# Turning the attention probabilities with VectorE block transposes and two DMA passes, in a one-core decoder layer

## The chip, the cores and the metric

One core of a Trainium2 chip runs the whole layer. The metric is the device time of one execution in microseconds (us), the median of several. The engines are TensorE (PE in the profile; its weight loads are PEld), VectorE (DVE), ScalarE (ACT), GpSimd (POOL) and SyncE (SP), which issues most of the DMAs.

## The reference

The layer is a selective scan over 128 positions, then a cross attention, then a linear layer, each behind a layer norm and with a residual. The change lies in the cross attention, with 8 batches, 128 queries, 128 keys, 32 heads of width 128 and a model width of 512:

```
h_q = (rmsnorm(z) @ w_q.T)      # z: the normed rows, 8 x 128 x 512
h_k, h_v = ctx @ w_k.T, ctx @ w_v.T
score = einsum('bqhd,bkhd->bhqk', h_q, h_k) + position_bias
score = softmax(where(mask, score, -inf))
attn  = einsum('bhqk,bkhd->bqhd', where(mask, score, 0), h_v)
out   = z + attn @ w_out.T
```

## The kernel before

**Two phases.** In the first some 380 us the scan runs on VectorE, ScalarE and GpSimd, while TensorE makes K and V of all heads and SyncE stores them in DRAM (k_dram, v_dram). The attention follows, and then the linear layer of some 25 us.

**Attention steps.** The attention is 64 steps: 32 heads times two halves of four batches (HB = 4, so a tile is 128 x 512). Head number g of these 64 is worked on over several steps, and each engine runs `step(g, ...)` in order. SyncE loads K and bias of g+1 (k_sb, bias, line 482), then V and the output weights of g (v_sb, wo_raw, line 485). TensorE makes the scores of g-1 (line 754), turns the probabilities of g-2 (line 778), adds the output product of g-3 to `misc` (lines 782 to 795: twelve 512-column matmuls, three for each product, since every float32 operand is split into a high and a low part), and multiplies V with the turned probabilities of g-2 (line 809). The matmul P.V contracts over the keys, so the probabilities, which softmax leaves with queries on the partitions, must stand with keys on the partitions. TensorE does this with four 128 x 128 transposes into the PSUM bank psT, and VectorE copies the bank to pt_sb (line 1344).

**Queries.** From step 10 on the query product is done for two heads at a time with seven half-size products instead of eight (`product`, six matmuls each, lines 686 to 688): W12, S2, S1 and S4 in an even step, S3, W11 and W22 in an odd one. Two PSUM areas, sumX and sumY, take turns, and VectorE and ScalarE combine them: q_u (u_sum), q_w (w_sum), and the four quarters of the queries c11 (ScalarE, line 1099), c12 (line 1366), c22 (line 1328) and c21 (line 1369). TensorE waits for c12 ahead of the scores of an odd step, and for c21 ahead of the product S2 of an even step.

**VectorE in one step.** q_u or c22; scores plus bias (line 1334, sb_done); maximum (line 1336); q_w; copy of the turned bank (line 1344); reciprocal of ScalarE's sum (line 1358); normalising (line 1360, p_ready); c12 or c21; low part of the head's output (line 1372, ot_lo).

**The others.** ScalarE takes c11, splits the weights (line 1104; line 1108 in odd steps; line 1084 for wo_hi), does four exponentials (line 1120), and last the high part of the head's output (line 1127, ot_hi) behind P.V. GpSimd makes the sums and low parts of the query weights (lines 1590 to 1605), the masked bias bm (line 1615) and wo_lo (line 1619).

## Time and profile before

| | |
|---|---|
| median of 3 runs | 909.33 us (909.28 to 910.69) |
| the profiled execution | 907.23 us, with a span of 905.4 us |
| PE busy | 896.5 us, 99% of the span |
| PEld, DVE, ACT, POOL busy | 86%, 77%, 57%, 74% of the span |
| granted TensorE clock | 1.00 throughout |
| DMA | 150.32 MB, mean 166 GB/s |

The span is the time from the first to the last instruction. An engine's busy share is a mean over stages; which engine sets the pace of a stage is read from who waits for whom.

### The profile page before, as it was taken

To read this page: it belongs to the slowest core of one execution; us is meant where nothing else is said; L and a number is where in the kernel's file an instruction comes from. 1 tells how busy PE (TensorE), PEld (TensorE's weight loads), DVE (VectorE), ACT (ScalarE), POOL (GpSimd) and SP (SyncE) were. 2 spreads that over 40 slices of the span, in tenths; PEclk is the share of its full clock that TensorE was granted. 3 is DMA by queue.
4 is the path that set the end of the run, shared out by engine and by line. 5 is a ranking of instruction groups with operands and counts; after the bars stand their busy time and mean duration, and the time that the engine had idled before them with its cause. 6 is when DMAs were issued, how large, how long until landed. Compare 5 with 4: busy or idle time off the path is not lost.

```text
span 905.4 us, 15443 instructions
## 1 busy us (share of the span) xinstructions
PE 896.5 (99%) x5146; PEld 776.4 (86%) x5146; DVE 694.7 (77%) x757; ACT 520.2 (57%) x1198; POOL 670.8 (74%) x437
## 2 busy tenths in 40 slices
PE   8999999999999999999999999999999999999998
PEld 7687888788888888888899999999899999999876
DVE  4799899999999997475666767676667676767774
ACT  3787867665666765456555555555555555555330
POOL 3245989997678795566788787888987878787522
PEclk9999999999999999999999999999999999999999
DMA  9454767576686762457445444444454544444302
GB/s 304 174 168 146 201 200 207 185 216 207 193 281 191 240 198 96 145 172 243 161 147 161 137 158 143 152 146 153 131 166 135 160 136 160 140 156 138 98 1 94
DMA packets 96913, 150.32 MB, mean 166 GB/s; under 512 B 10608, under 2 KB 35312, under 8 KB 96736
## 3 DMA queue, kind: packets, MB, share of 16 engines
q1 hardware_dynamic: 86496, 131.60, 44.4%
q10 hardware_dynamic: 10368, 18.09, 7.7%
q8 instruction: 28, 0.46, 0.2%
q14 instruction: 21, 0.17, 0.1%
HBM read 113.88 MB, written 35.78 MB: 165 GB/s over the span
## 4 chain that ended last, share of the span: by engine, by line
PE 85%; POOL 7%; DVE 4%; issue 2%; DMA 1%; ACT 1%; SPq 0%; ACTq 0%; DVEq 0%; POOLq 0%
PE acc L522 10%; PE acc L524 10%; PE acc L523 10%; PE misc L522 6%; PE misc L523 6%; PE misc L524 6%; PE acc L754 6%; PE acc L809 6%; PE acc L686 5%; PE acc L688 5%; PE acc L687 5%; PE acc L778 3%; POOL y L1538 2%; POOL wv_lo L1500 2%; DVE misc L1268 1%
## 5 line engine op out<-in xcount | busy, mean ns | idle before, releaser
L1538 POOL TENSOR_TENSOR y<-y,w 128x2048 f32<-128x2048 f32 x31 | 143.5, 4629 | 34.9 <-DVE w L1275 31.1
L1268 DVE TENSOR_TENSOR_SCAN misc<-dA,misc 128x2048 f32<-128x2048 f32 x32 | 141.7, 4429 | 4.9 <-ACT dA L881 1.7
L1120 ACT ACTIVATE prob<-prob,negm 128x128 f32<-128x128 f32 x256 | 99.9, 392 | 43.6 <-DVE negm L1336 43.6
L1127 ACT ACTIVATE ot_hi<-acc 128x512 fp32r<-128x512 f32 x64 | 38.3, 599 | 143.5 <-PE acc L809 143.5
L1602 POOL TENSOR_TENSOR wt_lo<-ws,wt_hi 128x1024 fp32r<-128x1024 f32 x27 | 65.2, 2414 | 61.6 <-ACT wt_hi L1108 59.4
L522 PE MATMUL misc<-wo_hi,ot_hi 128*128 128x512 f32 x256 | 107.3, 419 | 0.0
L522 PE MATMUL acc<-wv_hi,ctx_hi 128*128 128x512 f32 x256 | 100.4, 392 | 1.4 <-POOL wv_lo L1500 1.4
L524 PE MATMUL misc<-wo_hi,ot_lo 128*128 128x512 f32 x256 | 101.2, 395 | 0.0
L523 PE MATMUL misc<-wo_lo,ot_hi 128*128 128x512 f32 x256 | 101.1, 395 | 0.0
L1619 POOL TENSOR_TENSOR wo_lo<-wo_raw,wo_hi 128x512 fp32r<-128x512 f32 x64 | 95.9, 1499 | 6.3 <-ACT wo_hi L1084 6.3
L524 PE MATMUL acc<-wv_hi,ctx_lo 128*128 128x512 f32 x256 | 99.8, 390 | 0.0
L523 PE MATMUL acc<-wv_lo,ctx_hi 128*128 128x512 f32 x256 | 99.8, 390 | 0.0
L522 PE MATMUL acc<-ctx_hi,wk_hi 128*128 128x512 f32 x240 | 94.8, 395 | 0.0
L524 PE MATMUL acc<-ctx_hi,wk_lo 128*128 128x512 f32 x240 | 93.7, 390 | 0.0
L523 PE MATMUL acc<-ctx_lo,wk_hi 128*128 128x512 f32 x240 | 93.5, 390 | 0.0
L1360 DVE TENSOR_TENSOR prob<-prob,rec 128x512 f32<-128x512 f32 x64 | 88.6, 1384 | 2.2
L881 ACT ACTIVATE dA<-dt_,negA 128x508 f32<-128x508 f32 x128 | 89.2, 713 | 0.4 <-ACT xp_sb L996 0.4
L1372 DVE TENSOR_TENSOR ot_lo<-acc,ot_hi 128x512 fp32r<-128x512 f32 x64 | 44.3, 692 | 54.3 <-ACT ot_hi L1127 54.2
L1615 POOL TENSOR_TENSOR bm<-bias,maskadd 128x512 f32<-128x512 f32 x64 | 78.4, 1226 | 0.0
L1263 DVE TENSOR_TENSOR misc<-u,acc 128x2048 f32<-128x2048 f32 x32 | 73.5, 2297 | 4.9 <-ACT acc L897 1.7
L1275 DVE TENSOR_TENSOR w<-misc,bc 128x2048 f32<-128x2048 f32 x32 | 73.3, 2291 | 4.1
L859 ACT ACTIVATE kst<-acc 128x512 f32<-128x512 f32 x64 | 38.0, 598 | 60.6 <-PE acc L524 44.3
(206 smaller groups left out, 2448.2 us busy)
## 6 DMA issues: line engine op xcount, KB each, us to landing
k_scratch<-kst SPq DMA_DIRECT2D x64, 256.0 KB, 3.7
bc<-xp_scratch ACTq DMA_DIRECT2D x32, 512.0 KB, 5.6
v_scratch<-vst SPq DMA_DIRECT2D x32, 512.0 KB, 3.6
k_sb<-k_scratch SPq DMA_DIRECT2D x64, 256.0 KB, 2.7
v_sb<-v_scratch SPq DMA_DIRECT2D x64, 256.0 KB, 2.7
wo_raw<-in_wo SPq DMA_DIRECT2D x64, 256.0 KB, 2.9
wp<-in_wq SPq DMA_DIRECT2D x54, 256.0 KB, 3.7
wraw<-in_wk SPq DMA_DIRECT2D x32, 256.0 KB, 4.8
```

Source lines behind the costliest of these rows:

```text
L522: pe.matmul(out, w_hi, m_hi, start=first, stop=False)
L523: pe.matmul(out, w_hi, m_lo, start=False, stop=False)
L524: return pe.matmul(out, w_lo, m_hi, start=False, stop=last)
L881: act.activation(dA[k % 2][:, c, :, 1:S], dt_[:, half, c, :, 1:S], ACT.Exp, scale=negA[:, c, n:n + 1]).then_inc(da_ready, 1)
L1120: last = act.activation(prob[q][:, b], prob[q][:, b], ACT.Exp, bias=negm[q][:, b:b + 1], accum_out=psum[q][:, b:b + 1])
L1263: dve.tensor_tensor(misc[:, :, :], cols(u[:, half]), every(b_ps), ALU.mult).then_inc(dbx_done, 1)
L1268: dve.tensor_tensor_scan(h_ps, flat(dA[k % 2][:, :, :, :]), h_ps, 0.0, ALU.mult, ALU.add).then_inc(da_free, 1)
L1275: dve.tensor_tensor(cols(w[:, k % 2]), misc[:, :, :], every(bc[k % TRI][:, 1]), ALU.mult).then_inc(prod_done, 1)
L1360: dve.tensor_tensor(prob[q][:], prob[q][:], rec[q][:, :].unsqueeze(2).to_broadcast([P, HB, S]), ALU.mult).then_inc(p_ready, 1)
L1538: pool.tensor_tensor(y_half(half), y_half(half), w[:, k % 2], ALU.add).then_inc(y_ready, 1)
L1615: pool.tensor_tensor(bm[p][:], bias[p][:, :].unsqueeze(1).to_broadcast([P, HB, S]), maskadd[:, sh * HB:(sh + 1) * HB], ALU.add).then_inc(b ...
L1619: pool.tensor_tensor(wo_lo[p][:], wo_raw[p][:], wo_hi[p][:].bitcast(F32), ALU.subtract).then_inc(wo_lo_done, 1)
```

## The change

What it does:

- TensorE's four transposes (t_done), and VectorE's copy of their bank (pt_evac), go.
- Right behind normalising, VectorE transposes the 128 x 512 tile of probabilities in blocks of 32 x 32 within each group of 32 partitions (`turn`), into a new tile `blocks`.
- SyncE writes `blocks` to DRAM (one DMA of 256 KB) at the start of a step, ahead of the step's other loads. Behind the load of K and bias it waits for the write to have landed, and then reads it back with four DMAs of 64 KB, each into 32 partitions of pt_sb, in rows of 512 bytes, so that the blocks come to their transposed places.
- V and wo_raw are loaded one step later (for g-1).
- P.V moves one step later (g-3) and from the end of a step to a place ahead of the output product, which moves one step later too (g-4). ot_hi, ot_lo, split_wo and wo_lo follow. The pipeline has one step more at its end (STEPS + 4 steps).
- In an even step the product W12 now stands ahead of S2.
- The loads of the linear layer's weights go from SyncE at steps 4 to 6 to ScalarE's queue at steps 28 to 37. o_sum shares the memory of ea_sb. The transposes of the linear layer's first half (f_input) stand behind the output product of step 66 instead of at its start.

```diff
@@ SyncE, step
+                if runs(g - 2):
+                    sp.wait_ge(turned, g - 1)
+                    sp.dma_start(p_dram[p].rearrange("q j k x -> (q j) k x"),
+                                 blocks[p][:, :, :, :].rearrange("p k b i -> p k (b i)")).then_inc(blocks_out[p], 16)
...
                     load_kb(g + 1, head(g + 1, half), 1 - p)
-                if runs(g):
-                    if not known(g) or g >= 2:
-                        sp.wait_ge(pv_done, g - 1)
-                    sp.dma_start(v_sb[p][:, :, :].rearrange("p b d -> p (b d)"), v_dram[g]).then_inc(v_in[p], 16)
-                    if not known(g) or g >= 2:
-                        sp.wait_ge(wo_lo_done, g - 1)
-                    sp.dma_start(wo_raw[p][:], a["wo"][head(g, half)]).then_inc(wo_in[p], 16)
...
+                if runs(g - 2):
+                    sp.wait_ge(blocks_out[p], in_count(g - 2, p, 16))
+                    for k in range(4):
+                        sp.dma_start(pt_sb[p][32 * k:32 * (k + 1), :, :, :].rearrange("j q b i -> j q (b i)"),
+                                     p_dram[p, :, :, k].rearrange("q j x -> j q x")).then_inc(pt_in[p], 16)
+                if runs(g - 1):
+                    if not known(g) or g >= 3:
+                        sp.wait_ge(pv_done, g - 2)
+                    sp.dma_start(v_sb[1 - p][:, :, :].rearrange("p b d -> p (b d)"), v_dram[g - 1]).then_inc(v_in[1 - p], 16)
+                    if not known(g) or g >= 3:
+                        sp.wait_ge(wo_lo_done, g - 2)
+                    sp.dma_start(wo_raw[1 - p][:], a["wo"][(g - 1) % H if known(g) else g - 1 - H * half]).then_inc(wo_in[1 - p], 16)
@@ TensorE, step
                 elif paired(i) and not p:
+                    pe.wait_ge(s1_done, count(i))
+                    product(sumX, W12, pp, *z_of(half, 1, 0), False).then_inc(p2_done, 1)
                     pe.wait_ge(wc_lo, count(i))
                     if not known(i) or i > FIRST_PAIR:
                         pe.wait_ge(c21_done, count(i) - 1)
                     product(sumY, S2, pp, *t_of(half, T2), True).then_inc(p6_done, 1)
-                    pe.wait_ge(s1_done, count(i))
-                    product(sumX, W12, pp, *z_of(half, 1, 0), False).then_inc(p2_done, 1)
...
-                if runs(g - 2):
-                    pe.wait_ge(p_ready, g - 1)
...
-                    for b in range(HB):
-                        mm = pe.transpose(psT[:, b * S:(b + 1) * S], prob[p][:, b], ident[:])
-                    mm.then_inc(t_done, 1)
...
                 if runs(g - 3):
+                    pv(g - 3, 1 - p)
+                if runs(g - 4):
...
-                    pe.wait_ge(ot_lo_done, g - 2)
-                    pe.wait_ge(wo_lo_done, g - 2)
+                    pe.wait_ge(ot_lo_done, g - 3)
+                    pe.wait_ge(wo_lo_done, g - 3)
...
+            def pv(h, p):
+                pe.wait_ge(pt_in[p], in_count(h, p, 64))
+                pe.wait_ge(v_in[p], in_count(h, p, 16))
+                if known(h) and h == 0:
+                    pe.wait_ge(sum_evac, slot(NG, 0) - 1)
+                else:
+                    pe.wait_ge(ot_lo_done, h)
+                for b in range(HB):
+                    mm = pe.matmul(psO[:, b * S:(b + 1) * S].rearrange("p (q i) -> p q i", q=4), v_sb[p][:, b],
+                                   pt_sb[p][:, :, b], start=True, stop=True)
+                mm.then_inc(pv_done, 1)
@@ VectorE, step
-                    dve.tensor_copy(pt_sb[p][:, :, :].rearrange("p b q -> p (b q)"), psT).then_inc(pt_evac, 1)
...
                                       ALU.mult).then_inc(p_ready, 1)
+                    turn(g - 1, q)
...
+            def turn(h, q):
+                dve.wait_ge(p_ready, h + 1)
+                if not known(h) or h >= 2:
+                    dve.wait_ge(blocks_out[q], in_count(h - 2, q, 16))
+                dve.transpose(blocks[q][:, :, :, :].rearrange("p k b i -> p b k i"),
+                              prob[q][:, :, :].rearrange("p b (k j) -> p b k j", j=32)).then_inc(turned, 1)
```

## Rows read from the trace of the kernel before

**Rows 1.** Window: busy us of PE, PEld, DVE, ACT, POOL; clock; DMA share; GB/s.

```profile
700.00:800.00 100.00, 100.00 (x710) 92.87 (x710) 69.62 (x115) 53.90 (x166) 83.31 (x75) 1.00 0.49 153
```

**Rows 2.** Timeline of TensorE, one even and one odd step: start, duration in us.

```profile
720.87 0.36 PE L686 MATMUL acc<-tz,wt_hi 128*128 128x256 f32 x1
...
722.39 1.05 PE L754 MATMUL acc<-k_sb,q_sb 128*128 128x128 f32 x8
...
723.99 0.60 PE L778 MATMUL acc<-ident,prob 128*128 128x128 f32 x4
724.35 0.48 PE L522 MATMUL misc<-wo_hi,ot_hi 128*128 128x512 f32 x1
...
727.93 1.05 PE L809 MATMUL acc<-pt_sb,v_sb 128*128 128x128 f32 x8
728.74 0.36 PE L686 MATMUL acc<-tz,wt_hi 128*128 128x256 f32 x1
...
729.53 1.05 PE L754 MATMUL acc<-k_sb,q_sb 128*128 128x128 f32 x8
...
735.89 0.36 PE L686 MATMUL acc<-tz,wt_hi 128*128 128x256 f32 x1
```

**Rows 3.** Waits, 500 to 860 us: total us, times, longest us.

```profile
ACT ot_hi L1127 <- PE acc L809: 113.8, 48, 2.5
POOL wt_lo L1602 <- ACT wt_hi L1108: 54.4, 22, 2.6
```

**Rows 4.** Timeline of VectorE, an odd step and the even one behind it.

```profile
718.95 1.44 DVE L1360 TENSOR_TENSOR prob<-prob,rec 128x512 f32<-128x512 f32 x1
720.31 0.41 DVE L1369 TENSOR_TENSOR q_sb<-acc,q_s 128x256 f32<-128x256 f32 x1
...
723.48 0.69 DVE L1334 TENSOR_TENSOR prob<-acc,bm 128x512 f32<-128x512 f32 x1 [0.67 <-PE acc L754]
...
726.83 1.77 DVE L1360 TENSOR_TENSOR prob<-prob,rec 128x512 f32<-128x512 f32 x1
728.52 0.41 DVE L1366 TENSOR_TENSOR q_sb<-acc,q_u 128x256 f32<-128x256 f32 x1
```

**Rows 5.** Timeline of GpSimd in the same steps.

```profile
715.62 2.40 POOL L1602 TENSOR_TENSOR wt_lo<-ws,wt_hi 128x1024 fp32r<-128x1024 f32 x1 [2.58 <-ACT wt_hi L1108]
...
718.67 1.16 POOL L1615 TENSOR_TENSOR bm<-bias,maskadd 128x512 f32<-128x512 f32 x1
...
721.49 0.74 POOL L1590 TENSOR_TENSOR ws<-wp 128x256 f32<-128x256 f32 x1
...
726.76 1.29 POOL L1619 TENSOR_TENSOR wo_lo<-wo_raw,wo_hi 128x512 fp32r<-128x512 f32 x1
```

**Rows 6.** Two lines of VectorE: ns min/median/max, first and last start.

```profile
L1336 DVE TENSOR_REDUCE negm<-prob x64: 685/686/689, 384.6 to 859.3; 128x4 f32<-128x512 f32 x64
...
L1360 DVE TENSOR_TENSOR prob<-prob,rec x64: 691/1441/1814, 387.2 to 862.5; 128x512 f32<-128x512 f32 x64
```

**Rows 7.** Issue to landing: K's store (line 395, 256 KB), bias load (line 445, 64 KB).

```profile
DMA to landing us min/median/max: 2.0/3.7/8.4
...
DMA to landing us min/median/max: 2.2/3.0/6.3
```

**Rows 8.** Timeline of SyncE's queue: loads of K and bias.

```profile
724.34 0.33 SPq L444 DMA_DIRECT2D k_sb<-k_scratch  x1
724.87 0.33 SPq L445 DMA_DIRECT2D bias<-in_pbias  x1
```

**Rows 9.** Windows around the loads of V and wo_raw, and of K and bias.

```profile
721.00:724.30 3.30, 3.30 (x31) 3.30 (x30) 1.81 (x4) 2.31 (x5) 3.22 (x5) 1.00 0.48 159
724.30:729.00 4.70, 4.70 (x31) 4.16 (x30) 3.80 (x6) 1.67 (x9) 3.75 (x4) 1.00 0.25 70
```

**Rows 10.** Timeline of TensorE at the end: a weight sum, the linear layer's start.

```profile
866.91 1.98 PE L699 MATMUL acc<-eb_sb,ea_sb 128*128 128x512 f32 x4 [0.34 <-DVE ffn_w L1385]
...
877.30 0.39 PE L522 MATMUL acc<-weff_hi,zf_hi 128*128 128x512 f32 x1
```

More of the change, by code:

```diff
@@ L210, in decoder_layer @@
         prob = [sb(whole, f"prob{i}", [P, HB, S]) for i in pair]
-        pt_sb = [sb(whole, f"pt_sb{i}", [P, HB, S]) for i in pair]
+        pt_sb = [sb(whole, f"pt_sb{i}", [P, 4, HB, 32]) for i in pair]
         bm = [sb(whole, f"bm{i}", [P, HB, S]) for i in pair]
@@ L215, in decoder_layer @@
         ffn_w = sb(whole, "ffn_w", [P, C, D])
-        o_sum = sb(whole, "o_sum", [P, 2, D])
+        blocks = [sb(whole, f"blocks{i}", [P, 4, HB, 32]) for i in pair]
+        o_sum = ea_sb
         with ExitStack() as second_raw:
@@ L717, in step @@
                     weff_sum_of(2 * (g - STEPS))
-                if known(g) and g == STEPS + 2:
-                    f_input(0, (weff_sum, C), (sb_done, STEPS), (c21_done, count(PAIRS - 1)), (ot_lo_done, STEPS))
                 if plain(g):
@@ L795, in step @@
                     mm.then_inc(o_done, 1)
+                if known(g) and g == STEPS + 2:
+                    f_input(0, (weff_sum, C), (sb_done, STEPS), (c21_done, count(PAIRS - 1)), (ot_lo_done, STEPS))
                 if paired(i) and not p:
@@ L804, in step @@
                     v_sum(NG - 1, B - 1)
-                if runs(g - 2):
-                    pe.wait_ge(pt_evac, g - 1)
-                    pe.wait_ge(v_in[p], in_count(g - 2, p, 16))
-                    for b in range(HB):
-                        mm = pe.matmul(psO[:, b * S:(b + 1) * S], v_sb[p][:, b], pt_sb[p][:, b], start=True, stop=True)
-                    mm.then_inc(pv_done, 1)
+            def pv(h, p):
[9 more added lines that the diff above has]
+                mm.then_inc(pv_done, 1)
             def behind(g):
@@ L1122, in step @@
                     last.then_inc(exp_done, 1)
-                if runs(g - 2):
-                    act.wait_ge(pv_done, g - 1)
-                    if not known(g) or g > 3:
-                        act.wait_ge(o_done, g - 3)
-                    act.activation(ot_hi[p][:], psO, ACT.Copy).then_inc(ot_hi_done, 1)
+                if runs(g - 3):
+                    act.wait_ge(pv_done, g - 2)
+                    if not known(g) or g > 4:
+                        act.wait_ge(o_done, g - 4)
+                    act.activation(ot_hi[1 - p][:], psO, ACT.Copy).then_inc(ot_hi_done, 1)
+                if known(g) and H - 4 <= g < H:
+                    c = g - H + 4
+                    act.dma_start(ffn_w[:, c], a["ffn_w"][:, c]).then_inc(ffn_in, 16)
+                if known(g) and g == H:
+                    act.dma_start(ffn_b[:], a["ffn_b"].partition_broadcast(P)).then_inc(ffn_in, 16)
+                if known(g) and g == H + 5:
+                    act.wait_ge(x2_pool, 2)
+                    act.dma_start(ea_sb[:], a["ffn_a"]).then_inc(ffn_in, 16)
+                if known(g) and g == H + 1:
+                    act.dma_start(eb_sb[:], a["ffn_bw"]).then_inc(ffn_in, 16)
+                    for e in range(ER):
+                        act.dma_start(eprob[:, e:e + 1], a["probs"][P * e:P * (e + 1), :]).then_inc(ffn_in, 16)
                 if known(g) and g == STEPS:
```

65 lines of the change are left out of this document (25 added, 40 removed).

## The prediction

> **What bounds the kernel now.** I read three things in turn. First the busy time of a stretch of the attention [rows 1]: TensorE is busy for 100.00 of 100 us at the full clock, and VectorE (69.62) and GpSimd (83.31) are not. So a matmul that goes shortens the attention, as long as nothing else takes its place. Second the timeline of TensorE [rows 2], for what each block costs in pace and how long a pair of steps is: from 720.87, where an even step begins with the product S2, to 735.89, where the next one does, it is 15.02 us. Twenty-seven such pairs (heads 10 to 63) and ten heads of the plain form make up the attention. Third the timelines of VectorE and GpSimd [rows 4, 5], for how close behind TensorE the results come that it needs. They come very close. VectorE's c21 ends at 720.31 + 0.41 = 720.72, and TensorE uses it at 720.87. Its c12 ends at 728.52 + 0.41 = 728.93, and TensorE uses it at 729.53. The change makes TensorE quicker and puts work on VectorE just ahead of c12 and c21, so these two distances decide.
>
> **What TensorE saves.** The four transposes take 723.99 to 724.35, that is 0.36 us, and the matmul behind such a block of 128-column float32 matmuls takes 0.48 instead of 0.39 us, some 0.08 more [rows 2, 10]. P.V takes the transposes' place in front of the output product and pays the 0.08 there, but no longer does so in front of the next step. So a step saves 0.44 us, 64 steps save 28.2 us, and a pair would take 15.02 - 0.88 = 14.14 us. This is the most that the change can give, and one end of the range: 909.3 - 28.2 = 881.1 us.
>
> **What VectorE gets.** The trace has no block transpose. The nearest row is the maximum over the same 128 x 512 tile in SBUF, one source: 686 ns, with 685 and 689 as extremes, so GpSimd doesn't disturb it [rows 6]. The far bound is normalising, the same tile with two sources: 1,441 ns in the median [rows 6]. Below 0.69 us nothing on VectorE handles this many elements in float32 from these rows. I take 0.69, since it has one source. The copy that goes was off the path: it lay in the time of the exponentials. The Trainium skill, VectorE: DVE Perf Modes, The three transpose paths, gives 311 ns for a 128 x 128 bf16 transpose on VectorE; with three more tiles at one element per cycle of 0.96 GHz an estimate by that page is 0.71 us, and the sum would be the same within 0.02 us a step.
>
> **The two chains.** Chain A runs from the start of an even step's scores to the odd step's scores, through bias, maximum, exponentials, normalising and c12. Before, it takes VectorE 728.93 - 722.39 = 6.54 us and TensorE arrives after 7.14 us [rows 2, 4]. Chain B runs from the odd step's scores (729.53 - 15.02 = 714.51) to c21: 6.21 us, and TensorE arrives at S2 after 6.36 us.
> Now TensorE arrives on A after 7.14 - 0.44 = 6.70 us. On B it loses the transposes (0.36) and gains the product W12, which moves in front of S2: (1.52 - 0.08) / 2 = 0.72 us from 720.87 to 722.39; so 6.72 us. A, B and S2 (0.71) together are 14.13 us, which agrees with 14.14.
> With `turn` (0.69) and a hand-over of 0.07 us (VectorE starts 0.04 us behind the scores' end at 723.44 [rows 2, 4]; back to TensorE I allow a little more), A would take VectorE 7.30 us, 0.60 too long, and B 6.97 us, 0.25 too long. If nothing else changed, the saving would be gone: 14.13 + 0.85 = 14.98 us a pair.
>
> **Normalising gets shorter.** It takes 0.69 us alone (the shortest of 64) and 1.44 or 1.77 us here [rows 4, 6]. What is added is the rest of the GpSimd instruction that runs when it starts: it starts at 726.83, wo_lo ends at 728.05, and 0.69 later is 728.74 against an observed 728.60; in the odd step bm ends at 719.83, and 0.69 later is 720.52 against 720.39 [rows 4, 5]. So what counts is what GpSimd does then, and that shifts. Before, ScalarE waits up to 2.5 us for P.V with ot_hi, and behind it GpSimd waits up to 2.6 us for the split weights (L1602) [rows 3]. Now P.V of an even step begins 1.60 us behind its scores (where the transposes were, 723.99 - 722.39) and is over long before the exponentials, which end some 0.2 us ahead of normalising, 4.2 us behind the scores. From the end of P.V (728.98) to L1602 (715.62 + 15.02 = 730.64) it is 1.66 us, ot_hi and the split; counted from the exponentials' end L1602 starts at 4.2 + 1.66 = 5.9 instead of 8.25 us behind the even scores. From L1602 to the end of the odd step's wo_lo it is 3.05 + 1.16 + 1.29, so that ends at 11.4. The odd normalising starts at 6.72 + 4.44 = 11.16 and takes about 1.0 us. Then GpSimd, held off for 0.7, does what lay between 721.49 and 728.05 (6.56 us), and ends at 18.7, that is 4.3 us behind the next even scores: normalising there starts at 4.44 and takes about 0.7 us.
> Then A is 6.54 - 1.77 + 0.7 + 0.69 + 0.07 = 6.23 (needed after 6.70) and B is 6.21 - 1.44 + 1.0 + 0.69 + 0.07 = 6.53 (needed after 6.72). Both are covered by TensorE. What stays is thin: c12 must now wait for S4, which ends right in front of S3, so its 0.17 of matmul tail, 0.41 of work and hand-overs lie against the 0.71 of S3, and c21 stands the same way against W22 and W12. And GpSimd's place is known to some 0.3 us. I take a stall of 0.05 on A and 0.15 on B: 14.33 us a pair, 0.69 saved.
>
> **DMA.** A step gets one write of 256 KB and four reads of 64 KB. The turned odd head is ready at 11.16 + 1.0 + 0.69 = 12.9. The write is first in SyncE's step, where it waits for VectorE only; the query weights and K queued behind it aren't due, since K waits for sb_done at 14.33 + 1.09 + 0.69 = 16.1 anyway. It lands between 2.0 and 3.7 us later [rows 7], so by 16.7. K and bias are issued at 16.1 and 16.6, and the reads at 0.53 us each [rows 8], 17.2 to 18.8. The last lands 3.0 us later [rows 7], at 21.8. P.V of that head is at 14.33 + 6.72 + 1.60 = 22.65, so 0.9 us are left, and 0.2 if a read takes 3.7. V and wo_raw come behind, by 20.4, for a P.V more than a step later. The engines' load: K or V or wo_raw takes 0.48 x 3.3 / 2 = 0.79 us of all 16, K and bias 0.25 x 4.7 = 1.18, so 64 KB in 512-byte rows 0.39 [rows 9]. Added are 0.79 + 4 x 0.39 = 2.35 us to some 0.47 x 7.5 = 3.5, 5.85 of 7.17 us: 82%, busy but not full. I cost DMA at nothing; cover gone, each 0.1 us that a read is late beyond the 0.9 costs a pair 0.1.
>
> **Start, end and the rest.** The plain steps have no c12 or c21 and save the full 0.44 each: 4.4 us. P.V one step later makes the pipeline deeper, which moves work from the start to the end and adds none. At the end the last head's way from scores through the write (2.0 to 3.7) and reads (1.6 + 3.0) takes 4.44 + 1.0 + 0.69 + 2.0 to 3.7 + 4.6, 12.7 to 14.4 us. Beside it stand two P.V (0.80), two output products (2.9) and three weight sums of some 1.5 us [rows 2, 10], 12 us. So it costs 1 to 2 us; I take 1. The moved loads of the linear layer take ScalarE, which is half idle, a few issues.
>
> **Sum.** 27 x 0.69 + 4.4 - 1 = 22.0 us. Against the profiled execution, 907.2 becomes 885.2 and the span 905.4 becomes 883.4; the median of the runs lies 2.1 us above that execution, so I predict 887.3 us.
>
> **Rivals.**
> *Normalising stays as long.* For it: GpSimd is busy 83%, and in a shorter pair over 90%, so it is easy to meet. Against: the shift worked out above. A pair takes 14.98 us, and 27 x 0.04 + 4.4 - 1 = 4.5 us are saved: 904.8.
> *The reads land late.* For it: 0.9 us of room, and a queue that gets fuller, with reads behind K. Against: medians, not extremes, fill the room. With reads 1.5 us late each pair waits 0.6: 27 x 0.09 + 3.4 = 5.8 saved, 903.5. From 1.8 us late on it is slower than before.
> *The block transpose is dear (slower than before).* At normalising's 1.44 us, with normalising short, A misses by 0.28 and B by 0.56, a pair takes 14.97, and it is 905. With normalising as long as before A misses by 1.35 and B by 1.0: 16.5 us a pair, 27 x 1.46 - 3.4 = 36 us slower, 945. The turning point is 0.77 us per transpose with long normalising, 1.5 us with short. For it: no row of VectorE shows a float32 tile crossing partitions. Against: the 0.69 of every one-source row. In the same page of the Trainium skill, Rules for kernel authors gives TensorE the 128 x 128 transpose and VectorE only the 32 x 32 one; by that rule the change would go this way, and no row here shows it.
>
> **Chances.** The forecast (881 to 896) 0.50, normalising as long 0.14, late reads 0.16 (of it 0.05 slower), a dear transpose 0.17 (of it 0.11 slower), something not seen 0.03. What a measurement here tells from no change is 0.2%, 1.8 us. Faster 0.78, same 0.05, slower 0.17. The range reaches from the full saving, 880, to 911, beyond the two rivals at 905. The forecast's own is 881 to 896.
>
> **What would show it.** Right: no line for the transposes; `turn` at some 690 ns; line 1360 at a median under 1.1 us; a pair of 14.1 to 14.5 us; ScalarE's wait for P.V gone; reads that land ahead of P.V. Wrong: TensorE waiting for c21 (S2) or c12 (odd scores) by 0.5 us or more, which is the long normalising or a long `turn`, or waiting ahead of P.V for pt_sb.

## The result, and the profile after

The changed kernel takes 904.99 us (median of 6 runs, 903.06 to 906.27), the kernel before in the same comparison 909.31: a ratio of 0.9952, with a 95% interval of 0.9939 to 0.9965. It is faster, but by 4.3 us where 22.0 were predicted. The profiled execution took 903.9 us, its span is 902.1 us against 905.4.

The window that [rows 1] shows of before, 700 to 800 us, in the same columns:

```profile
700.00:800.00 100.00, 98.84 (x667) 89.69 (x665) 62.76 (x117) 54.67 (x174) 83.66 (x76) 1.00 0.72 221
```

TensorE is no longer busy all the time: 1.16 us of 100 are idle. The clock is full. The DMA share went from 0.49 to 0.72. The parts of VectorE's work that the prediction priced, from the lines of the changed kernel (ns min/median/max):

```profile
L1369 DVE TENSOR_TENSOR prob<-prob,rec x64: 691/694/1822, 386.9 to 856.2; 128x512 f32<-128x512 f32 x64
...
L1389 DVE STREAM_TRANSPOSE blocks<-prob x64: 711/711/716, 387.6 to 858.0; 128x512 f32<-128x512 f32 x64
```

The block transpose costs 0.71 us, and normalising fell from a median of 1.44 [rows 6] to 0.69. Both are as forecast. The wait of ScalarE for P.V [rows 3] is no longer among the waits over 1.4 us of that stretch. What waits from 500 to 860 us:

```profile
POOL wt_lo L1620 <- ACT wt_hi L1110: 34.1, 21, 1.9
...
PE acc L810 <- DMA pt_sb<-p_scratch: 3.5, 4, 1.7
...
PE acc L754 <- issue: 2.8, 11, 0.7
```

No row says that TensorE waits for VectorE's c12. Yet the pair is long. TensorE's timeline over an odd head's scores (705.10), the even step's end and the next scores (712.20):

```profile
704.32 0.35 PE L688 MATMUL acc<-tz,wt_hi 128*128 128x256 f32 x1
...
705.10 1.05 PE L754 MATMUL acc<-k_sb,q_sb 128*128 128x128 f32 x8
...
706.70 1.05 PE L810 MATMUL acc<-pt_sb,v_sb 128*128 128x128 f32 x8
707.51 0.47 PE L524 MATMUL misc<-wo_hi,ot_hi 128*128 128x512 f32 x1
...
710.39 0.27 PE L688 MATMUL acc<-z_hi,wt_hi 128*128 128x256 f32 x1
...
710.98 0.28 PE L690 MATMUL acc<-z_hi,wt_lo 128*128 128x256 f32 x1
711.10 0.28 PE L688 MATMUL acc<-tz,wt_hi 128*128 128x256 f32 x1
...
711.69 0.28 PE L690 MATMUL acc<-tz,wt_lo 128*128 128x256 f32 x1
712.20 0.80 PE L754 MATMUL acc<-k_sb,q_sb 128*128 128x128 f32 x5 [0.23 <-issue]
```

The same stretch on VectorE, from the even step's normalising on:

```profile
709.63 0.69 DVE L1369 TENSOR_TENSOR prob<-prob,rec 128x512 f32<-128x512 f32 x1
710.47 0.71 DVE L1389 STREAM_TRANSPOSE blocks<-prob 128x512 f32<-128x512 f32 x1
711.39 0.42 DVE L1376 TENSOR_TENSOR q_sb<-acc,q_u 128x256 f32<-128x256 f32 x1 [0.20 <-PE acc L690]
```

S4 (the row at 710.98 is its last) ends at 711.26, the transpose at 711.18. c12 (L1376) starts behind both, at 711.39, and ends at 711.81. S3, from 711.10, is all that TensorE has meanwhile; its last matmul starts at 711.69 and hands the array on after 0.12. The scores start at 712.20, 0.39 after c12. From 705.10 to 712.20 are 7.10 us, where TensorE's own work is 6.70 and 6.75 were predicted. The pair from 697.52 to 712.20 is 14.68 us; over ten pairs, from the scores of head 40 (682.86) to those of head 60 (829.21), it is 14.64 on average, against 15.02 before and 14.33 predicted. The short steps (chain A) are 6.98 to 7.10 there but for one of 6.72, the long ones (chain B and S2) mostly 7.58 to 7.68, where 7.58 were predicted. So what is too long is mainly A.

The start of the pipeline is worse. P.V of head 1, in step 4:

```profile
405.65 2.08 PE L810 MATMUL acc<-pt_sb,v_sb 128*128 128x128 f32 x8 [4.11 <-DMA pt_sb<-p_scratch]
407.38 0.77 PE L524 MATMUL misc<-wo_hi,ot_hi 128*128 128x512 f32 x1
...
408.80 0.63 PE L524 MATMUL misc<-wo_hi,ot_hi 128*128 128x512 f32 x1
...
411.24 0.39 PE L524 MATMUL misc<-wo_hi,ot_hi 128*128 128x512 f32 x1
```

TensorE waits 4.11 us for the reads, and then its matmuls take 0.63 instead of 0.39 us until 411. Windows of that stretch (the clock is the third figure from the end):

```profile
404.00:406.00 2.00, 0.35 (x1) 0.35 (x2) 2.00 (x2) 0.00 (x0) 2.00 (x2) 0.57 0.59 170
406.00:408.00 2.00, 2.00 (x10) 1.90 (x10) 1.39 (x3) 0.54 (x3) 1.23 (x1) 0.50 1.02 280
408.00:410.00 2.00, 2.00 (x6) 1.60 (x5) 0.82 (x2) 2.00 (x8) 0.00 (x0) 0.50 0.85 314
```

The granted clock is 0.50 there, the level of 1.2 GHz. P.V and nine matmuls take 405.65 to 411.24, 5.59 us; the same in a steady step (706.70 to 709.69) takes 2.99. So the low clock costs 2.6 us beside the wait.

**Where the 18.7 us of span are that are missing.** Between the scores of head 10 (457.84 before, 457.83 after) and those of the last head (857.52, 851.50) 6.0 us were saved. The forecast for these 26.5 pairs was 26.5 x 0.69 = 18.3: 12.3 are missing, of them 26.5 x (14.64 - 14.33) = 8.2 in the steady pair and 4.1 in irregular steps. About half of these 4.1 lie between the scores of heads 32 and 40: that takes 61.61 us, before 61.10, and four pairs shorter by 0.38 would make it 59.6. From the first scores (382.73, 382.43) to head 10 it takes 75.11 us before and 75.40 after: 0.3 lost where 4.4 were to be saved, 4.7 missing. From the last scores to the end it is 47.9 before and 50.6 after, 2.7 instead of 1: 1.7 missing.

### The profile page after: what moved, and what is told of

The parts are those of the page before. It is cut to its first block, busy times and chain, and to the rows that moved or that the text cites. A ratio compares the mean times of both kernels' runs of the same rounds, so it can differ in the third digit from the quotient of the medians.

```text
span 902.1 us, 15211 instructions
## 1 busy us (share of the span) xinstructions
PE 880.7 (98%) x4890; PEld 753.4 (84%) x4890; DVE 667.8 (74%) x757; ACT 515.3 (57%) x1198; POOL 668.2 (74%) x437
## 4 chain that ended last, share of the span: by engine, by line
PE 75%; POOL 9%; DMA 6%; DVE 4%; issue 3%; SPq 2%; ACT 1%; ACTq 0%; DVEq 0%; POOLq 0%
PE acc L524 10%; PE acc L526 10%; PE acc L525 10%; PE misc L524 6%; PE misc L525 6%; PE misc L526 6%; PE acc L810 6%; PE acc L754 5%; PE acc L688 4%; PE acc L689 4%; PE acc L690 4%; POOL y L1556 2%; DMA p_scratch<-blocks 2%; DMA pt_sb<-p_scratch 2%; POOL wv_lo L1518 2%
## 5 line engine op out<-in xcount | busy, mean ns | idle before, releaser
L1620 POOL TENSOR_TENSOR wt_lo<-ws,wt_hi 128x1024 fp32r<-128x1024 f32 x27 | 64.7, 2397 | 37.4 <-ACT wt_hi L1110 34.6
L1637 POOL TENSOR_TENSOR wo_lo<-wo_raw,wo_hi 128x512 fp32r<-128x512 f32 x64 | 85.3, 1334 | 8.4 <-ACT wo_hi L1086 8.4
L1367 DVE RECIPROCAL rec<-psum 128x4 f32<-128x4 f32 x64 | 11.4, 178 | 97.1 <-ACT prob L1122 97.1
L810 PE MATMUL acc<-pt_sb,v_sb 128*128 128x128 f32 x512 | 69.4, 279 | 8.4 <-DMA pt_sb<-p_scratch 8.4
L1348 DVE TENSOR_TENSOR prob<-acc,bm 128x512 f32<-128x512 f32 x64 | 44.2, 691 | 43.1 <-PE acc L754 43.0
L754 PE MATMUL acc<-k_sb,q_sb 128*128 128x128 f32 x512 | 69.5, 278 | 4.4 <-issue 3.0
```

The lines of the kernel that those rows point to most:

```text
L754: mm = pe.matmul(psS[:, b * S:(b + 1) * S], q_sb[1 - p][:, b * S:(b + 1) * S], k_sb[1 - p][:, b * S:(b + 1) * S], start=True, stop=True)
L810: mm = pe.matmul(psO[:, b * S:(b + 1) * S].rearrange("p (q i) -> p q i", q=4), v_sb[p][:, b], pt_sb[p][:, :, b], start=True, stop=True)
L1637: pool.tensor_tensor(wo_lo[1 - p][:], wo_raw[1 - p][:], wo_hi[1 - p][:].bitcast(F32), ALU.subtract).then_inc(wo_lo_done, 1)
```

## Experiments

All ratios are to the kernel before in the same comparison; that of the changed kernel is 0.9952. Where two kernels are compared, the difference is that of their ratios times 909 us.

### The pair: what holds c12

Two edits, each alone and then both. The first puts S4 and W22 between the second and the third part of the output product instead of behind the fourth:

```python
                if runs(g - 4):
                    ...
                    for b in range(2):
                        out_part(g, h, q, b)
                if paired(i) and not p:
                    pe.wait_ge(w_sum, count(i))
                    product(sumX, S4, pp, *z_of(half, 1, 1), False).then_inc(p3_done, 1)
                elif paired(i):
                    ...
                if runs(g - 4):
                    for b in range(2, HB):
                        mm = out_part(g, h, q, b)
```

> S4 (even step) and W22 (odd step) run between the second and the third of the four output products instead of behind the fourth, 1.4 us earlier; nothing else differs from the changed kernel. My theory is that c12 is held by S4's end, at 711.26, and by the transpose in front of it on VectorE, which ends at 711.18, and then pays 0.39 us of hand-over to TensorE, with S3 alone to cover it. With S4 early only the transpose still holds c12: it starts at about 711.20 instead of 711.39, 0.2 us a pair or 5 us in all: about 900 us, ratio to the kernel before about 0.990. Rival 1, S4's end alone holds it (the transpose isn't in the way): the whole stall goes, 10 us, about 894. Rival 2, the missing gain lies in transfers, contention or the clock: no change, 905.

Measured: 901.41 us, 0.9900 (0.9883 to 0.9917), 4.7 us less than the changed kernel. The second edit moves the transpose:

```diff
-                    turn(g - 1, q)
                 if paired(i) and not p:
                 ...
                     dve.tensor_tensor(q_sb[1][:, 0:HALF_T], sumY, q_s1[pp][:], ALU.add).then_inc(c21_done, 1)
+                if runs(g - 1):
+                    turn(g - 1, q)
```

> The block transpose moves behind c12 and c21 on VectorE (still ahead of ot_lo); TensorE's order stays. My theory: c12 still waits for S4's end, so it starts no earlier than 711.26; 0 to 1 us faster than the changed kernel, 904 to 905 us. Rival 1, the transpose alone is in the way: 5 to 10 us faster, 895 to 900. Rival 2, no part of it: no change, or slower by late reads (the write leaves 0.4 us later), 905 to 910.

Measured: 905.42 us, 0.9964 (0.9949 to 0.9978): no gain; the ratio is 1.1 us worse, within the two intervals.

> Both edits: S4 and W22 between the output products, the transpose behind c12 and c21. My theory: only now is nothing in front of c12 and c21; both chains run into their start with more than 0.4 us to spare, so the pair falls from 14.68 us to TensorE's own work, 14.2, 27 times 0.45 = 12 us: about 893 us, ratio 0.982. The two edits are worth more together than their sum. Rival 1, hand-over and transpose are not what holds the pair: 905. Rival 2, either edit is enough alone: this one equals the better of the two.

Measured: 897.29 us, 0.9858 (0.9834 to 0.9883), 8.5 us less than the changed kernel where the two edits alone give 4.7 and nothing. The steady pair is 14.13 us (7.43 + 6.70) from 485 us on, but for the middle of the run. In its trace c12 no longer waits for TensorE:

```profile
708.43 1.48 DVE L1375 TENSOR_TENSOR prob<-prob,rec 128x512 f32<-128x512 f32 x1
709.83 0.41 DVE L1381 TENSOR_TENSOR q_sb<-acc,q_u 128x256 f32<-128x256 f32 x1
710.16 0.69 DVE L1396 STREAM_TRANSPOSE blocks<-prob 128x512 f32<-128x512 f32 x1
```

Normalising is at its long value here, c12 ends at 710.24 and the scores start at 710.60 all the same. The ten pairs from head 40 to head 60 show what each edit is worth without the start and the middle of the run:

| kernel | scores of head 40 | of head 60 | us per pair |
|---|---|---|---|
| before | 684.47 | 834.67 | 15.02 |
| changed | 682.86 | 829.21 | 14.64 |
| S4 and W22 earlier | 685.50 | 828.50 | 14.30 |
| transpose behind c12 and c21 | 684.93 | 831.09 | 14.62 |
| both | 682.34 | 823.67 | 14.13 |

The changed pair has 0.50 us beyond the 14.13 of the last row. The place of S4 and W22 is the main holder: moving them alone takes 0.34 away. The transpose ends within 0.1 us of S4 and stands in its shadow: moving it alone gives 0.02, since c12 still waits for S4, and it is worth 0.17 once S4 is early. The whole gains less than the pairs. With S4 early 26.5 pairs give 9 us and the median 4.7; with both, 13 and 8.5. In both traces the first scores come 3.6 us later (386.00 and 386.05 instead of 382.43) and the step in the middle of the run is longer (11.56 and 10.10 instead of 8.65); what stands behind this is read at the end of the part on the start.

The price of time in front of c12 and c21:

```diff
+                dve.tensor_reduce(spare[:], prob[q][:], AX_X, ALU.max)
                 dve.transpose(blocks[q][:, :, :, :].rearrange("p k b i -> p b k i"),
```

> A second tensor_reduce of the normalised probabilities (about 0.69 us, its output unused) is put in front of every block transpose. It prices the time in front of c12 and c21. My theory: their slack against the transpose's end is 0.1 to 0.2 us in either step, so 0.5 us are lost on both, 27 pairs times 1.0 = 27 us: about 932 us. Rival, VectorE has room there (transfers or the clock set the pair): 905 to 910.

Measured: 919.95 us, 1.0123 (1.0100 to 1.0146), 15.5 us slower than the changed kernel: there is no room in front of c12 and c21, as stated, but at little more than half the size. The pairs of its trace are mostly 15.0 to 15.9 us, 0.3 to 1.2 longer, not 1.0 each.

### The hand-over

TensorE waits for K's load and for sb_done behind its waits for c11 and c12. This run turns that round:

```diff
+                    pe.wait_ge(kb_in[1 - p], in_count(g - 1, 1 - p, 32))
+                    if not known(g) or g > 1:
+                        pe.wait_ge(sb_done, g - 1)
+                    else:
+                        pe.wait_ge(dbx_done, NSTEP)
                     if plain(g - 1):
                         pe.wait_ge(q_evac, g)
                     elif p:
                         pe.wait_ge(c11_done, count(i))
                         pe.wait_ge(c12_done, count(i))
                     else:
                         pe.wait_ge(c21_done, count(i) - 1)
-                    pe.wait_ge(kb_in[1 - p], in_count(g - 1, 1 - p, 32))
...
```

> The changed kernel with one order of waits changed: ahead of each head's scores TensorE waits first for K's load and sb_done and last for q_evac, c11/c12 or c21, instead of the other way round. In the changed kernel's trace c12 ends at 711.81 and the scores' first matmul starts at 712.20 (weight load 712.17), 0.36 to 0.39 us later, put down to issue, while S2, whose wait for c21 stands directly in front of it, starts 0.05 to 0.10 us behind c21. Theory: the two waits behind c12's, one of them against a computed value, are the hand-over; with c12's last the scores start 0.1 us behind it, the pair loses 0.25 to 0.3 us less, 27 times: 7 to 8 us, 897 to 898, pairs of 14.3 to 14.4. Rival: the hand-over belongs to the weight load of q_sb, which c12 writes: no change, 904 to 905, pairs stay at 14.6 to 14.7.

Measured: 901.67 us, 0.9919 (0.9892 to 0.9945). VectorE's c12 and TensorE's scores in its trace:

```profile
710.94 0.42 DVE L1376 TENSOR_TENSOR q_sb<-acc,q_u 128x256 f32<-128x256 f32 x1 [0.20 <-PE acc L690]
```

```profile
711.51 0.68 PE L754 MATMUL acc<-k_sb,q_sb 128*128 128x128 f32 x4
```

The scores start 0.15 us behind c12's end (711.36) instead of 0.39, and the short step is 6.77 to 6.86 instead of 6.98 to 7.10. So 0.24 us of the hand-over came with two waits for things that had already happened, standing behind the one that had not; the rival, the weight load of q_sb, is out, since that load is still there. The gain, 3.0 us, is less than the 7 to 8 expected. The pair from head 40 to head 60 is 14.47 us instead of 14.64, so 26.5 pairs give 4.4; and the step at the middle of the run took 10.79 us in this trace and 8.65 in that of the changed kernel.

### The order of W12 and S2

```diff
-                    pe.wait_ge(s1_done, count(i))
-                    product(sumX, W12, pp, *z_of(half, 1, 0), False).then_inc(p2_done, 1)
                     pe.wait_ge(wc_lo, count(i))
...
                     product(sumY, S2, pp, *t_of(half, T2), True).then_inc(p6_done, 1)
+                    pe.wait_ge(s1_done, count(i))
+                    product(sumX, W12, pp, *z_of(half, 1, 0), False).then_inc(p2_done, 1)
```

> The changed kernel with S2 ahead of W12 again, as in the kernel before; all else as changed. Theory: W12 ahead of S2 is the cover of c21 (W22's end to S2), 0.72 us; without it S2 waits for c21 with nothing between, 0.7 to 0.9 us a pair, 27 times: 20 to 24 us slower than the changed kernel, 925 to 929, slower than the kernel before. Rival: c21 isn't on the chain that sets the pair (c12 alone is): 905.

Measured: 919.16 us, 1.0118 (1.0103 to 1.0134), 15 us slower than the changed kernel. From 460 to 860 us TensorE waits for c21:

```profile
PE acc L688 <- DVE q_sb L1379: 16.3, 26, 1.1
```

That is 0.6 us in each of 26 pairs; the pair from head 40 to head 60 is 15.37 us. c21's chain needs W12 in front of S2 as cover.

### P.V behind S4 and W22

```diff
-                if runs(g - 3):
-                    pv(g - 3, 1 - p)
...
                     product(sumY, W22, pp, *t_of(half, T4), False).then_inc(p4_done, 1)
+                if runs(g - 3):
+                    pv(g - 3, 1 - p)
```

> On the changed kernel, P.V moves from ahead of the output product to the end of TensorE's step, behind S4 and W22, where the kernel before had it; nothing else. My theory (c12 and c21 pay 0.39 us of hand-over behind S4 and W22 with one product to cover it) says that P.V's 0.81 us covers it: the pair falls from 14.68 to 14.1 or 14.2, and the reads have 3.6 us more to land, so P.V's waits for them go too (4.1 at the start, 3 to 5 later): 888 to 895. Rival: ot_hi and ot_lo, now behind the end of the step, hold VectorE ahead of the next score's bias add, the softmax comes later and the write with it: 900 to 915.

Measured: 913.70 us, 1.0061 (1.0047 to 1.0075), slower than before. P.V stands in front of S3 and W12 again as cover, but now the other thing that holds c12 and c21 grew: the pair from head 40 to head 60 is 15.10 us, and from 460 to 860 us the scores wait 6.6 us for c12 and S2 6.7 us for c21. VectorE in an odd step, and S2 on TensorE:

```profile
705.98 1.45 DVE L1369 TENSOR_TENSOR prob<-prob,rec 128x512 f32<-128x512 f32 x1
707.57 0.71 DVE L1389 STREAM_TRANSPOSE blocks<-prob 128x512 f32<-128x512 f32 x1
708.20 0.38 DVE L1379 TENSOR_TENSOR q_sb<-acc,q_s 128x256 f32<-128x256 f32 x1
```

```profile
708.64 0.39 PE L688 MATMUL acc<-tz,wt_hi 128*128 128x256 f32 x1 [0.21 <-DVE q_sb L1379]
```

Normalising is long again (median 1,387 ns). As read from this trace and not tested alone, P.V's late place moves ot_hi and so GpSimd's order of work back, and ot_lo (701.67, behind ot_hi) stands in front of the next head's bias add. Long normalising and transpose together make c12 and c21 late. The test is the same kernel with the transpose out of the way:

> As before this one, and the block transpose behind c12 and c21. If the P.V product covers the hand-over by itself, this adds nothing (within 2 us of the other); if the transpose still stands in front of c12, it gains as it did with the split output product, 3 to 5 us more.

Measured: 892.46 us, 0.9822 (0.9809 to 0.9836): 22 us less for moving one 0.7 us instruction, which gave nothing in the changed kernel's own order. The pair is 14.14 to 14.16 us, though normalising is still long in half of the steps (median 1,078 ns), and from 460 to 860 us there is one wait for reads (3.0 us).

### The start

> On the changed kernel, SyncE issues each block's write ahead of the plain steps' W_q load, and in step 3 ahead of the last v_scratch store too (in the changed kernel the store, 512 KB, and W_q, 256 KB, go out in front of the second write, which leaves at 396.51, 0.65 us behind the transpose, takes 1.32 to issue and lands some 5.7 us after it). My theory: the pipeline's start is held by that write; it lands 2 to 3 us earlier, P.V in step 4 waits 1 to 2 us instead of 4.1, and with less of the slow stretch behind it the kernel gains 2 to 5 us: 900 to 903. Rival: the reads, or the K load ahead of them, hold P.V, or what is gained comes back as another wait of the same stretch: 904 to 906.

Measured: 903.41 us, a ratio of 0.9956 (0.9938 to 0.9975), no change. In the trace steps 4 and 5 take 10.11 + 8.80 = 18.91 us instead of 14.17 + 7.33 = 21.50; TensorE now waits 2.55 us for ot_lo there, and the clock stays at 1.00. So the write's landing is one holder, with VectorE's order close behind. The filler:

```diff
+                if known(g) and g == 4:
+                    pe.wait_ge(sum_evac, slot(NG, 0))
+                    for k in range(36):
+                        pe.transpose(psY[:, 0:S], ident[:], ident[:])
                 if runs(g - 3):
                     pv(g - 3, 1 - p)
```

> On the changed kernel, 36 transposes of the identity (their output unused) stand on TensorE ahead of P.V in step 4, where it now idles for 4.11 us; they take 0.10 to 0.12 us each, so 3.6 to 4.3 us. The wait for the reads stays; only TensorE's granted clock can differ. In the changed kernel's trace the clock behind the idle stretch is 0.50 to 0.73 of full speed (the level of 1.2 GHz) from 405 to 411. Theory: the idle stretch brings that on, and with the filler the matmuls behind it take 0.39 instead of 0.63 us: 2 to 3 us faster, 902 to 903. Rival: the clock falls for another reason (or the matmuls slow down with the transfers): no gain, 905 or more.

Measured: 907.74 us, 0.9990 (0.9973 to 1.0006), slower than the changed kernel. But the windows of its trace show what it was to show:

```profile
404.00:406.00 2.00, 2.00 (x21) 2.00 (x20) 1.97 (x4) 1.37 (x3) 1.55 (x2) 1.00 0.49 137
406.00:408.00 2.00, 2.00 (x18) 1.91 (x16) 2.00 (x3) 0.00 (x0) 2.00 (x2) 1.00 1.02 256
```

With TensorE kept busy the clock stays at 1.00, with transfers as heavy as before (1.02), and the matmuls of 128 x 512 take 0.39 us. So here the low clock goes with the idle stretch ahead of them, not with the transfers. Steps 4 and 5 take 19.39 us, 2.1 less. The next four steps give 2.9 us back (8.22, 7.93, 8.99 and 6.78 against 7.32, 7.62, 7.32 and 6.79), and the step at the middle of the run took 13.09 against 8.65. Two more runs move VectorE's z_lo out of the first steps, in the changed kernel and in the fastest:

```diff
-                if g in (1, 2):
+                if g in (5, 9):
```

> The changed kernel with VectorE's z_lo of the second half (two pieces of 2.9 us behind steps 1 and 2, between a transpose and the next score's bias add) moved behind steps 5 and 9. Theory for the start: VectorE is in step with TensorE only from head 4 on; its first heads follow each other at 7.5 us (388.28 to 391.09 is z_lo), while TensorE starts its scores every 5.4 to 6.4, so blocks, write and reads of head 1 come late and P.V in step 4 waits. With z_lo out of the way head 1's bias add comes 1.5 us earlier and head 2's 4 us: the wait of 4.1 us shrinks to 2 or less and with it the slow stretch: 2 to 4 us faster, 901 to 903. Rival: write and reads alone hold it: 904 to 905.

Measured: 905.18 us, 0.9967 (0.9949 to 0.9985).

> The fastest kernel so far (P.V late, transpose behind c12/c21, W_o a step later: 888.5 us) with the same move of z_lo. There TensorE idles in step 4 for ot_lo of head 0, which stands in VectorE's order behind head 2's softmax, itself late by z_lo. Theory: 2 to 4 us faster, 885 to 887; if the start is held otherwise: 888 to 889.

Measured: 889.48 us, 0.9797 (0.9780 to 0.9815). In both traces the start is shorter: the first five scores take 29.2 us instead of 32.2 (6.35 + 6.34 + 4.56 + 11.96) in the first, steps 4 and 5 take 17.37 instead of 19.30 in the second. In both it is given back where the pieces went: in the second, steps 10 and 11 take 8.09 + 9.13 instead of 6.72 + 7.57, 2.9 us. So VectorE's order is the start's other holder; where z_lo would cost nothing was not found.

**What one trace can show of the start and the middle.** The traces also differ where no edit touches them. The five kernels that keep the changed kernel's start (S4 and W22 earlier, the transpose behind, both, the waits turned round, S2 first) take 19.59 to 20.62 us for steps 4 and 5, against 21.50 in the changed kernel's trace. So gains of 2 to 3 us against that one trace are in good part spread. Clear of it are the 18.91 us of the early write and, with P.V late, 17.37 against 19.30 to 19.57. And the time of the first scores goes from 382.43 to 386.05 us. The same window of the scan phase, in the trace of the early write and in that of the changed kernel:

```profile
38.00:40.00 2.00, 2.00 (x5) 1.61 (x6) 1.93 (x3) 1.97 (x4) 0.00 (x0) 0.50 0.51 179
```

```profile
38.00:40.00 2.00, 2.00 (x11) 1.61 (x10) 1.84 (x3) 1.97 (x4) 0.00 (x0) 1.00 0.90 192
```

In the first trace the granted clock is 0.50 to 0.53 from 38 to 44 us, behind eight small matmuls of 16 rows that take 4 us (33.88 to 38); in the second the clock stays at 1.00 behind the same matmuls. The first scores then come at 385.92 instead of 382.43, 3.5 us later, which is more than the 2.9 us that the first ten heads gain (72.52 against 75.40). The step in the middle goes the same way. P.V waits there for its reads, and behind the wait the clock can fall, as in the filler's trace:

```profile
666.17 2.08 PE L814 MATMUL acc<-pt_sb,v_sb 128*128 128x128 f32 x8 [3.37 <-DMA pt_sb<-p_scratch]
```

```profile
669.00:672.00 3.00, 3.00 (x9) 2.32 (x8) 0.29 (x1) 0.83 (x1) 3.00 (x3) 0.50 0.64 165
```

With the clock at 1.00 that step took 7.87, 8.65 and 10.10 us, behind waits of 0.9 (z_lo later), 1.66 (changed) and 3.11 us (both edits); with the clock falling to 0.50 it took 10.79, 11.56 and 13.09, behind 2.20 (waits turned round), 3.01 (S4 earlier) and 3.37 us (filler). The length of the wait alone doesn't decide it, since the clock fell behind 2.20 us and not behind 3.11.

### SyncE's queue

> On the kernel with both edits (split output products, transpose behind c12 and c21; it measured 897.3 us, ratio 0.986), the four reads are issued ahead of K's load and the bias rather than behind them. The waits of P.V for its reads in the middle of the run (5.3 us between 600 and 820, 12.2 us in all with the start's 4.4) are the question. Theory: the reads leave 1 to 2 us earlier and these waits go, 3 to 5 us faster: about 893. Rival: the reads then make SyncE wait for the write's landing with K's load queued behind them, so scores wait for K: slower by up to 0.5 us a step, 900 to 925. Second rival, neither: the late reads come from the write, and nothing changes.

Measured: 986.60 us, 1.0860 (1.0826 to 1.0894), far beyond the price that either side had given. SyncE's waits over the whole trace:

```profile
SPq L491 <- DMA p_scratch<-blocks: 248.0, 64, 7.3
```

In each step the queue stands 3.9 us on average for the write's landing, with K, bias, V and W_o behind it; the pair is 17.60 us on average from head 40 (730.77) to head 60 (906.72). In the changed kernel that wait is 31.0 us in all, since the wait for sb_done and K's load fill it. So the reads' place behind K's load is a part of the change that must stay.

> Both edits on TensorE and VectorE, and the write ahead of W_q and of the last store as in the other run of this call. If the start's wait and the pair's hand-over are separate losses, their gains add: 897.3 less 2 to 5 us, 892 to 895. If the start's stretch is held by something else, 896 to 898.

Measured: 897.23 us, 0.9878 (0.9856 to 0.9901), the same as without the early write. Its trace shows the middle of the run, where GpSimd adds the first half's sums. SyncE, then GpSimd, then TensorE:

```profile
641.93 0.43 SPq L502 DMA_DIRECT2D v_sb<-v_scratch  x1
646.52 0.35 SPq L505 DMA_DIRECT2D wo_raw<-in_wo  x1
646.92 0.43 SPq L476 DMA_DIRECT2D p_scratch<-blocks  x1
```

```profile
636.98 2.56 POOL L1672 TENSOR_TENSOR base<-base,ea_sb 128x512 f32<-128x512 f32 x2 [3.96 <-ACT ea_sb L1181]
...
645.21 1.28 POOL L1646 TENSOR_TENSOR wo_lo<-wo_raw,wo_hi 128x512 fp32r<-128x512 f32 x1
```

```profile
656.20 1.34 PE L818 MATMUL acc<-pt_sb,v_sb 128*128 128x128 f32 x8 [2.78 <-DMA pt_sb<-p_scratch]
```

GpSimd waits 3.96 us for ScalarE, so wo_lo ends at 646.49, and W_o's load, which waits for it, stands 4.1 us in front of the write. Before the change only loads stood behind W_o; now the probabilities do. The run that loads W_o a step later, behind the next write:

```diff
                                  blocks[p][:, :, :, :].rearrange("p k b i -> p k (b i)")).then_inc(blocks_out[p], 16)
+                    if not known(g) or g >= 4:
+                        sp.wait_ge(wo_lo_done, g - 3)
+                    sp.dma_start(wo_raw[p][:], a["wo"][(g - 2) % H if known(g) else g - 2 - H * half]).then_inc(wo_in[p], 16)
...
-                    if not known(g) or g >= 3:
-                        sp.wait_ge(wo_lo_done, g - 2)
-                    sp.dma_start(wo_raw[1 - p][:], a["wo"][(g - 1) % H if known(g) else g - 1 - H * half]).then_inc(wo_in[1 - p], 16)
```

> On the kernel with split output products, the transpose behind c12/c21 and the early write (897.2 us): W_o of a head is loaded one step later, behind the next write, so SyncE no longer waits for GpSimd's wo_lo in front of the write. In that kernel's trace the step at the middle of the run (step 38, where GpSimd adds the first half's sums) takes 11.3 us instead of 7.43, SyncE waiting there up to 4 us for wo_lo. Theory: that wait is what delays the write and the reads; the step falls to 7.5 to 9, 2 to 4 us faster: 893 to 895. Rival: the write waits for something else there (K's load, the transpose), no change: 897.

Measured: 892.43 us, 0.9831 (0.9810 to 0.9852), 4.3 us less than with the early load of W_o. The step in the middle still takes 9.46 us (11.34 without the edit), P.V waits 2.5 us there (2.8 without) and the clock stays at 1.00 (0.51 from 657 to 660 without). So the wait for its reads got little shorter; the later load gains, but how much of it by the queue's wait, by the load's place and by the clock isn't separated.

### The two repairs together

> P.V at the end of the step and the transpose behind c12/c21 (892.5 us), with W_o loaded one step later, behind the next write. If the wait of SyncE for wo_lo at the middle of the run is a loss of its own, the two steps there (10.05 and 8.87 us in that kernel's trace instead of 7.43 to 8) shrink by 2 to 4 us: 889 to 890. If with P.V late that wait no longer reaches TensorE: 892 to 893.

Measured: 888.49 us, 0.9786 (0.9766 to 0.9806), the fastest kernel by its median: P.V behind S4 and W22, the transpose behind c12 and c21, W_o a step later. Most of its gain over the same kernel with the early W_o load lies in step 34, which takes 7.43 us instead of 10.05, with P.V's wait for its reads at 0.5 instead of 3.0 us. There the queue didn't wait for wo_lo (1.1 us in all from 600 to 665, at a later step). W_o's load (624.82) went out in front of the write (625.29), and the reads followed the write by 5.9 us (631.15); with the load behind the write they follow by 3.4 (627.63 and 631.07). So in this order the gain goes with the load's place in front of the write, not with its wait; one trace of each is all that shows it.

> As the other of this call, and the second write ahead of W_q and of the last store at the start. In the kernel with P.V late TensorE idles 3.1 us in step 4 for ot_lo of head 0, which VectorE runs behind head 3's normalise, not for the reads: if that order on VectorE is what holds the start, the early write is worth nothing (within 1 us of the other). If the write's landing holds it, 2 to 3 us faster.

Measured: 889.53 us, 0.9802 (0.9780 to 0.9824), the same: beside VectorE's order the write's landing isn't what holds the start there.

## Why the prediction was wrong

**Right.** TensorE's saving: with c12 and c21 out of the way the pair is 14.13 to 14.16 us, where the full saving of 0.88 gave 14.14. The transpose: 0.71 us for 0.69. Normalising: 694 ns in the median for 0.7 and 1.0, by the mechanism given: ScalarE's wait for P.V went from 113.8 to 0.4 us, and GpSimd's split weights (L1620) start 5.79 us behind the even scores where 5.9 were worked out (8.25 before). The stall on B: 0.15 were taken, and the long steps have 0.15 to 0.25 beyond 7.43. W12 as cover of c21: without it 15 us are lost. The danger was in the text, too: "What stays is thin: c12 must now wait for S4, which ends right in front of S3".

**Wrong, the step that decides: "I take a stall of 0.05 on A and 0.15 on B".** On A the stall is 7.10 - 6.70 = 0.40, in other pairs from 0.28 on. The term was mis-sized in its hand-over. The "hand-over of 0.07 us" came from VectorE's start behind TensorE, and c12's way back to the scores was never seen as a wait before, since there TensorE came 0.60 us behind c12 [rows 2, 4]. It takes 0.39 us here, 0.24 of it the waits behind c12's in the code. Worked out from the rows of after: S4's tail 0.16, VectorE's start 0.13, c12 0.42 and 0.39 make 1.10 us from the pass of S4's last matmul on; 0.71 of it is S3, and 0.39 is the stall. The prediction set 0.17 + 0.41 and its 0.07 of hand-over, 0.65 in all, against S3's 0.71 and so saw a fit; the hand-over was 0.13 + 0.39. Before, P.V's 0.81 us lay there as well and hid it. Moving S4 and W22 alone takes 0.34 of the pair's 0.50 away (the short steps are then 6.69 to 6.76 us), and putting c12's wait last 0.17, so this cause is tested. The steady pairs are 8.2 of the 18.7 us.

**Wrong: "I cost DMA at nothing" and "makes the pipeline deeper, which moves work from the start to the end and adds none".** In the steady pair the reads do land in time, as said. At the start they don't: the deeper pipeline empties the first steps, TensorE comes early, and then waits 4.1 us for head 1's blocks and runs 2.6 us longer at half the clock. The end took 2.7 us where one step's P.V and output product (0.80 + 2.9) plus 1 would be 4.7, so the start should have gained 8.1 us; it lost 0.3 here, and the best trace of a kernel with the same start gained 2.0 (73.15 us for the first ten heads against 75.11 before). That the plain steps "save the full 0.44 each" holds from step 5 on (7.33 against 7.77 us).

**Wrong in the irregular steps.** The reads' 0.9 us of room was worked out for a steady pair. The queue's waits at the middle of the run weren't looked at, and there the write stands behind W_o's load and its wait for GpSimd (2.9 us in the changed kernel, once). About half of the 4.1 us lies there; the later W_o load gives 4.3 us in one order and 3.3 in the other (0.9786 against 0.9822).

**The rivals.** 904.8 (normalising stays long) and 903.5 (reads late in each pair) are near the result by size, but that is chance and neither is what happened: normalising was short, and from 500 to 860 us P.V waited for its reads four times, 3.5 us in all. The dear transpose didn't come either. The rule of the Trainium skill that was weighed for it (VectorE: DVE Perf Modes, Rules for kernel authors) gives a 128 x 128 transpose to TensorE. These runs go the other way: the work that moved off TensorE was worth its 0.88 us a pair once VectorE's transpose stood where nothing waited.

**Open.** Why the granted clock falls behind a wait in one execution and not in another: the traces show where it fell and what that cost, not the reason. Why four steps behind the filler are longer by 2.9 us. How the start's 8.4 us (8.1 due, 0.3 lost) divide: the early write and the later z_lo each show a holder, but no kernel here gets them back. And the rest of the hand-over, 0.15 us, was not taken apart.

## What to carry to other kernels

A product that stands between a wait's source and its user is cover: when it moves, look at each hand-over that it covered, and measure a hand-over at the place where it is used, with every wait that the code puts behind the decisive one. Put the wait that is fulfilled last at the end of the list, and work for later (here a transpose whose result is due a step later) behind the results that the pace-setting engine waits for. When data that is needed at once goes through a queue that used to carry loads with time to spare, every wait ahead of it in that queue has become part of the chain. And price an edit in the stretch that it touches, over several pairs and traces: a total also holds clock falls that come and go from one execution to the next.

## What the runs showed of the hardware

- A float32 block transpose of 128 x 512 on VectorE takes 711 ns, nearly alike in all 64 cases (711 to 716), 25 ns more than the maximum over the same tile.
- The granted clock was 0.50 behind TensorE's idle 4.11 us at 401.5 to 405.7, and was at 1.00 again from about 411.2 on; with transposes in the gap it stayed at 1.00, under a DMA share of 1.02. After the 2.55 us of the early write's run it stayed at 1.00 as well, and after 3.11 us in the run with both edits; after 2.20 us in the run with the waits turned round it fell to 0.50.
- The granted clock can differ between executions of the same instructions: 0.50 to 0.53 from 38 to 44 us in one trace, 1.00 in another, and the first scores 3.5 us apart.
- TensorE's waits for conditions that are already true aren't free where they stand behind the decisive one: two of them, one against a computed value, took 0.24 us in front of the scores, and the profile puts it down to issue, not to a wait.
- SyncE's issue of the blocks' write is 0.33 us in the median, but up to 1.70; it is 1.32 us at 396.51, behind a store of 512 KB and a load of 256 KB.
